# The first stage of a quantized FFN kernel: conditioning of block 1 moved into the first product, and three smaller rearrangements

## What is computed

```python
c = einsum('bct,bcd->bdt', x, cond_weights[cond])      # x: (128, 64, 512)
h = gelu(einsum('bsd,hd->bsh', c, ternarize(W1)) + b1) # W1: (2048, 512)
y = einsum('bsd,hd->bsh', h, ternarize(W2)) + b2       # W2: (512, 2048)
scale = max|y| / 7 + 1e-8
out = x + clip(round(y / scale), -7, 7) * scale

def ternarize(W):
    delta = 0.05 * max|W|;  mask = |W| > delta
    n = max(sum(mask), 1);  alpha = sum(|W| where mask) / n
    return alpha * sign(W) * mask
```

## Time and profile before

| | |
|---|---|
| median of 3 runs | 1014.92 us (1014.45 to 1015.22) |
| profiled execution | 1013.76 us |
| its span | 1012.0 us |
| PE busy | 928.2 us, 92% |
| DVE busy | 647.5 us, 64% |
| ACT busy | 546.2 us, 54% |
| mean granted clock of PE | 0.97 |

### The profile page before, as it was taken

The page is one execution under the profiler, slowest core; times in us unless marked ns, Lnnn a source line. Parts: engine busy times, 40 slices in busy tenths (PEclk is TensorE's granted clock), DMA queues, the critical chain, the costliest instruction groups (busy, mean ns, idle before and its releaser), DMA issues.

```text
span 1012.0 us, 14566 instructions
## 1 busy us (share of the span) xinstructions
PE 928.2 (92%) x5088; PEld 439.1 (43%) x5088; DVE 647.5 (64%) x1025; ACT 546.2 (54%) x688; POOL 145.4 (14%) x187
## 2 busy tenths in 40 slices
PE   2899999999999999999999999999999999999600
PEld 2354444444444444444444444444444444444200
DVE  7999666566667666665667666565666665633492
ACT  5685826455472827446372827446372826535290
POOL 1420030210303030110303030110303030000000
PEclk9999999999999999999999999999999999999855
DMA  9401201111210301121210301121210301105899
GB/s 347 136 9 38 46 11 42 47 47 41 52 41 17 76 10 41 46 47 41 52 41 10 83 10 41 45 48 41 52 41 10 75 18 42 42 0 201 300 394 391
DMA packets 24317, 77.85 MB, mean 77 GB/s; under 512 B 3952, under 2 KB 4080, under 8 KB 23792
## 3 DMA queue, kind: packets, MB, share of 16 engines
q1 hardware_dynamic: 20032, 73.41, 24.1%
q0 software_dynamic: 3840, 3.94, 1.4%
q10 hardware_dynamic: 432, 0.34, 0.1%
HBM read 60.89 MB, written 16.78 MB: 77 GB/s over the span
## 4 chain that ended last, share of the span: by engine, by line
PE 83%; issue 9%; DVE 4%; ACT 1%; DMA 1%; DVEq 0%; POOL 0%; POOLq 0%
PE ps L426 41%; PE ps L436 36%; PE ps L491 3%; PE ps L406 3%; ACT y L680 1%; DVE st L814 1%; DVE wts L1017 1%; DMA condb<-in_itok_B 1%; DVE y L1017 0%; DVE y L833 0%; PE ps L414 0%; PE ps L454 0%; DVE yc L746 0%; DVEq L58 0%; DVE st L697 0%
## 5 line engine op out<-in xcount | busy, mean ns | idle before, releaser
L426 PE MATMUL ps<-yc,wts 128*128 128x512 f16 x2048 | 446.3, 380 | 3.6 <-DVE yc L746 3.6
L436 PE MATMUL ps<-wts 128*128 128x512 f16 x1792 | 391.4, 379 | 0.0
L426 PEld LDWEIGHTS ps<-yc,wts 128*128 128x128 f16 x2048 | 200.7, 98 | 246.8 <-DVE yc L746 4.1
L730 DVE SCALAR_TENSOR_TENSOR wts<-g,st,wts 128x512 f16<-128x512 f32 x256 | 186.3, 749 | 144.0 <-ACT wts L593 142.4
L588 ACT ACTIVATE g<-ps,b1t,st 128x512 f32<-128x512 f32 x256 | 197.9, 773 | 129.0 <-PE ps L426 120.7
L436 PEld LDWEIGHTS ps<-wts 128*128 128x128 f16 x1792 | 173.4, 98 | 204.9
L593 ACT ACTIVATE wts<-g,st 128x512 f16<-128x512 f32 x256 | 180.8, 712 | 0.0
L575 ACT ACTIVATE xs<-yx,st 128x2048 f16<-128x2048 f32 x28 | 56.1, 2002 | 135.5 <-DVE st L764 135.5
L359 POOL PARTITION_ALL_REDUCE st<-st x46 | 22.7, 494 | 672.5 <-DVE st L699 412.7
L343 POOL DMA_INDIRECT wg<-in_L_cond_weights,ids x112 | 110.0, 982 | 41.5 <-issue 29.1
L735 DVE SCALAR_TENSOR_TENSOR y<-ps,st,b2b 128x512 f32 (+1 forms) x56 | 41.6, 747 | 78.9 <-PE ps L436 78.1
(11 more groups left out here) (127 smaller groups left out, 359.3 us busy)
## 6 DMA issues: line engine op xcount, KB each, us to landing
yx<-in_x SPq DMA_DIRECT2D x56, 512.0 KB, 6.2
out<-wts SPq DMA_DIRECT2D x12, 512.0 KB, 14.9
wts<-in_x SPq DMA_DIRECT2D x10, 512.0 KB, 5.6
y<-in_L_ffn_W SPq DMA_DIRECT2D x8, 512.0 KB, 8.6
wts<-in_x SPq DMA_DIRECT2D x4, 1024.0 KB, 5.2
y<-in_L_ffn_W SPq DMA_DIRECT2D x4, 1024.0 KB, 18.5
y<-in_x SPq DMA_DIRECT2D x4, 1024.0 KB, 10.7
out<-y SPq DMA_DIRECT2D x4, 1024.0 KB, 15.3
```

The costliest lines, as they stand in the source:

```text
L426: last = nc.tensor.matmul(psH[:, j % HB, :], T1T[:, j // HC, k, j % HC * P:(j % HC + 1) * P], csp[:, a, k, :], start=(k == 0 and a == 0), ...
L436: last = nc.tensor.matmul(psY[:, r % 2, :], hsp[:, a, j, r * P:(r + 1) * P], T2T[:, j, :], start=(j == 0 and a == 0), stop=(j == HT - 1 an ...
L730: nc.vector.scalar_tensor_tensor(out=hsp[:, 1, j, :], in0=g[:, j % HB, :], scalar=s_h, in1=hsp[:, 0, j, :], op0=ALU.mult, op1=ALU.subtract ...
```

## The change

It edits the first stage on all engines:

- DVE: the two memsets (`wdirect`, `twos`) go ahead of the wait for the conditions.
- x of block 0 is bounded by a sum of absolute values over each partition, made by ACT (`ACT.Abs` with `accum_out`), in place of DVE's maximum. The all-reduce on POOL waits for it (`x0_summed`). A factor in `mr[:, 1:2]` follows from the new bound.
- POOL: two of the four gathers for block 1 go right behind those of block 0, two behind the all-reduce of W1's maximum. SP: x of block 1 is loaded ahead of W2.
- PE: block 1 is conditioned behind j = 0 of block 0's first product, into the banks that block 0's conditioning used; its copy goes to a place of its own (`cf1`) and is made by ACT after tiles 3 and 5. Behind the first product only waits remain.
- PE: `count2` takes W2's negatives (`neg2`) as the stationary operand in 64 pieces of 128 columns and one column of the constant as the moving one; the result is one column.
- ACT: `relu1` and `spread_w(1)` are ordered anew; the first pair of `relu2` goes inside `hidden(0)` after j = 11, the others directly behind it, and `high_c(1)` behind those.
- DVE: two `ternary1` go ahead of the scale of h, the maxima of W2 alternate with `low_h`, `scale_xw` goes to the end of the alpha2 sequence, and `low_x(0, 0)` behind the stores and maxima of y of block 0.

The diff, cut to these parts:

```diff
@@ sync
             load_direct(0)
+            load_direct(1)
             load_weight(w2s, W2.rearrange("p j n -> p (j n)"), WCH, w2_loaded)
-            load_direct(1)
             load_half(0, 2 * DIRECT)
@@ gpsimd
-            gather_direct(0)
+            gather_direct(0, range(RT))
+            gather_direct(1, range(0, 2))
...
             all_max(max1_part, 1, m1r, m1, max1_all)
+            gather_direct(1, range(2, RT))
+            pool.wait_ge(x0_summed, 1)
             all_max(xwb_part, 1, xwbr, xwb, xwb_all)
-            gather_direct(1)
...
             all_max_c(1)
-            all_max(xw_part, 1, xwr, xw, xw_all)
             pool.wait_ge(sum2_part, 1)
             nc.gpsimd.partition_all_reduce(sum2r, sum2, P, RADD).then_inc(sum2_all, 1)
+            all_max(xw_part, 1, xwr, xw, xw_all)
@@ tensor
             def count2(c):
-                for n in range(WCH):
-                    last = nc.tensor.matmul(psN2, twos[:, :], quarter(neg2, c, n), start=(c == 0 and n == 0),
-                                            stop=(c == WCH - 1 and n == WCH - 1))
+                for n in range(QUARTER // P):
+                    at = c * QUARTER + n * P
+                    last = nc.tensor.matmul(psN2, neg2[:, at:at + P], twos[:, 0:1], start=(c == 0 and n == 0),
+                                            stop=(c == WCH - 1 and n == QUARTER // P - 1))
...
                 first(0, j, wait_bank=j >= HB, wait_c=False)
-
-            pe.wait_ge(xdirect_loaded[1], 16)
-            pe.wait_ge(w_spread, 2)
-            condition_direct(1, 0, psC)
-            pe.wait_ge(g_made, HT - 2)
-            condition_direct(1, 1, psC1)
-
+                if j == 0:
+                    pe.wait_ge(xdirect_loaded[1], 16)
+                    pe.wait_ge(w_spread, 2)
+                    condition_direct(1, 0, psC)
+                    condition_direct(1, 1, psC0)
+
+            pe.wait_ge(c_copied, 2)
             pe.wait_ge(g_made, HT)
@@ scalar
+            nc.scalar.activation(dump_x, xdirect[0].rearrange("p r t -> p (r t)"), ACT.Abs, accum_out=xwb[:, 0:1])\
+                .then_inc(x0_summed, 1)
...
-            hidden(0, lambda j: spread_w(1) if j == 3 else None, wait_c=False)
-            act.wait_ge(delta2_ready, 1)
-            act.wait_ge(t1_made, WCH)
-            for side in range(2):
-                relu2(0, side)
-            act.wait_ge(h_split, HT)
-            copy_c_direct(1, 0, psC[:, :, :])
-            copy_c_direct(1, 1, psC1)
+            def beside_first(j):
+                if j in (3, 5):
+                    copy_c_direct(1, (j - 3) // 2, (psC, psC0)[(j - 3) // 2])
+                if j == 11:
+                    act.wait_ge(delta2_ready, 1)
+                    act.wait_ge(t1_made, WCH)
+                    for side in range(2):
+                        relu2(0, side)
+
+            hidden(0, beside_first, wait_c=False)
@@ vector
-            dve.wait_ge(xdirect_loaded[0], 16)
-            nc.vector.tensor_reduce(xwb[:, 0:1], xdirect[0], AX.XY, ALU.max, apply_absolute_value=True).then_inc(xwb_part, 1)
...
-            ternary1(1)
+            ternary1(3)
             low_h(0, 0)
-            ternary1(2)
-            low_h(0, 1)
...
+            for c in range(WCH):
                 last = max_w2(c)
+                low_h(0, 2 * c + 1)
+                if c < WCH - 1:
+                    low_h(0, 2 * c + 2)
...
-            low_x(0, 0)
+            scale_xw(0, 0, link)
             dve.wait_ge(b2_loaded, 16)
...
             for r in range(RT):
                 max_y(0, r, tile_y(r), slot(r), wait_last=r > 0)
+            low_x(0, 0)
             hidden_step(0, link, False)
```

More of the change, by code:

```diff
@@ L132, in build @@
         w1s, w1abs, w2s = flat(y[:, 0:4, :, :]), flat(y[:, 4:8, :, :]), flat(y[:, 8:12, :, :])
-        mask1, neg2, dump2 = f16(y[:, 12:14, :, :]), f16(y[:, 4:6, :, :]), f16(y[:, 0:4, :, :])
+        mask1, neg2, dump2 = f16(y[:, 12:14, :, :]), f16(y[:, 6:8, :, :]), f16(y[:, 0:4, :, :])
         t1_flat, t2_flat = wts[:, 0:KT * H], wts[:, KT * H:2 * KT * H]
@@ L143, in build @@
         cf = g[:, :, :]
+        cf1 = y[:, 4, :, :]
+        dump_x = hsp[:, 0, 0:RT, :].rearrange("p j r -> p (j r)")
         def place(ap):
@@ L181, in build @@
         n1, n1c, sm1, alpha1, alpha1p = stat(), stat(), stat(), stat(), stat()
-        rs2, at2 = stat(2 * WCH), stat(WCH)
+        rs2, at2 = stat(2 * WCH), stat(WCH + 1)
         sum2, sum2r = stat(2), stat(2)
@@ L185, in build @@
         cinv = stat(2)
-        n2n, n2, n2c, sm2, alpha2 = stat(), stat(), stat(), stat(), stat()
+        n2c, sm2, alpha2 = stat(), stat(), stat()
         pm, ms, mr = stat(KT), stat(2), stat(2)
@@ L199, in build @@
         psC0 = psY[:, :, :].rearrange("p i (k r) -> p (i k) r", k=KT // 2)
-        psC1 = psH[:, 0:2, :].rearrange("p i (k r) -> p (i k) r", k=KT // 2)
-        psN1, psN2 = psH[:, HB - 1, :], ps[:, HB, :]
+        psN1, psN2 = psH[:, HB - 1, :], ps[:, HB, 0:1]
         psY0 = [psY[:, 0, :], psY[:, 1, :], psH[:, 2, :], psH[:, 3, :]]
@@ L219, in build @@
         xwb_part, xwb_all = sem("xwb_part"), sem("xwb_all")
+        x0_summed = sem("x0_summed")
         mask1_made = sem("mask1_made")
@@ L345, in gather, with gather_direct @@
                         in_offset=bass.IndirectOffsetOnAxis(ap=ids[:, j:j + 1], axis=0)).then_inc(w_gathered[j // HALF], 16)
-            def gather_direct(b):
-                for r in range(RT):
+            def gather_direct(b, tiles):
+                for r in tiles:
                     nc.gpsimd.indirect_dma_start(
@@ L484, in _ @@
                 if j == 3 * HC:
-                    pe.wait_ge(c_copied, 1)
                     for c in range(WCH):
@@ L557, in copy_c_direct @@
                 act.wait_ge(c_made, 2 * b + half + 1)
-                nc.scalar.activation(cf[:, :, half_rows(half)], bank, ACT.Copy).then_inc(c_copied, 1)
+                nc.scalar.activation(cf1[:, :, half_rows(half)], bank, ACT.Copy).then_inc(c_copied, 1)
             def high_c0(half, bank):
@@ L576, in high_x, with high_c @@
                 nc.scalar.activation(ws[:, 0, js, :], wg[:, js, :], ACT.Copy, scale=sxw[:, 1:2]).then_inc(xhi_made, 1)
-            def high_c(b):
+            def high_c(b, cf=cf):
                 act.wait_ge(cscale_ready, b + 1)
@@ L622, in relu2 @@
                                      accum_out=rs2[:, 2 * c + side:2 * c + side + 1]).then_inc(relu2_summed, 1)
-            for c in range(6):
+            for c in range(LOADS):
                 absolute(c)
+            act.dma_start(b2b[:, :], b2.rearrange("(a n) -> a n", a=1).to_broadcast([P, T])).then_inc(b2_loaded, 16)
             act.wait_ge(diagonal_cleared, 1)
             spread_w(0)
-            for c in range(6, LOADS):
-                absolute(c)
-            act.dma_start(b2b[:, :], b2.rearrange("(a n) -> a n", a=1).to_broadcast([P, T])).then_inc(b2_loaded, 16)
+            act.wait_ge(xdirect_loaded[0], 16)
+            nc.scalar.activation(dump_x, xdirect[0].rearrange("p r t -> p (r t)"), ACT.Abs, accum_out=xwb[:, 0:1])\
+                .then_inc(x0_summed, 1)
             act.wait_ge(delta1_ready, 1)
             act.wait_ge(w1abs_made, LOADS)
-            for c in range(3):
-                relu1(c)
+            relu1(0)
             high_c0(0, psC)
             high_c0(1, psC0)
+            relu1(1)
+            act.wait_ge(c_made, 2)
+            spread_w(1)
+            relu1(2)
             relu1(3)
             act.wait_ge(relu_summed, WCH)
-            hidden(0, lambda j: spread_w(1) if j == 3 else None, wait_c=False)
-            act.wait_ge(delta2_ready, 1)
-            act.wait_ge(t1_made, WCH)
-            for side in range(2):
-                relu2(0, side)
-            act.wait_ge(h_split, HT)
-            copy_c_direct(1, 0, psC[:, :, :])
-            copy_c_direct(1, 1, psC1)
[L649 to L652, removed]
+            def beside_first(j):
[7 more added lines that the diff above has]
+            hidden(0, beside_first, wait_c=False)
+            for c in range(1, WCH):
                 for side in range(2):
                     relu2(c, side)
+            act.wait_ge(h_summed, HT)
+            high_c(1, cf1)
             high_x(0, 0)
@@ L693, in bits, with max_c @@
                 return ap.bitcast(I32)
-            def max_c(b, lk):
+            def max_c(b, lk, cf=cf):
                 dve.wait_ge(c_copied, 2 * b)
@@ L716, in scale_h, with low_c @@
                 nc.vector.tensor_scalar(ascale, pc, 2.0 / TOP, alpha1, ALU.mult, ALU.mult).then_inc(hscale_ready, 1)
-            def low_c(b):
+            def low_c(b, cf=cf):
                 dve.wait_ge(cscale_ready, b + 1)
@@ L796, in _ @@
             link(nc.vector.tensor_tensor(pc64, upper, pcol, ALU.add))
+            nc.vector.memset(wdirect, 0.0).then_inc(diagonal_cleared, 1)
+            nc.vector.memset(twos[:, :], 2.0).then_inc(consts_made, 1)
             dve.wait_ge(cond_loaded, 16)
@@ L841, in _ @@
             mask_w1(0)
```

(49 more changed lines are left out.)

2 lines of the change are left out of this document (removed).

## The result

The changed kernel takes 1020.68 us (median of 4 runs, 1020.26 to 1021.5) against 1014.68 for the kernel before (4 runs): ratio 1.0067, 95% interval 1.0055 to 1.008, so 5.6 to 8.1 us slower. The ratio is not the quotient of these two medians (1.0059): it agrees with the mean of these 4 runs over that of the 19 runs of the kernel before that stand beside the first experiments (median 1013.84). The profiled execution took 1020.87 us, 7.11 more than the one before.

The account below looks back on a forecast made before the run. The prediction took TensorE, busy 92% of the span, to bound the kernel nearly everywhere. It summed +0.4 - 1.6 + 5.25 + 1.3 = +5.35 us, giving 1020.3 us against the median of 1014.92, range 1016.0 to 1024.0.

Parts of the forecast that it names:

- Likeliest case: Whole kernel: all terms as summed, 1020.3 us, own range 1018 to 1022.5; chance 0.60.
- start of the second product: Block 0: second product starts at 66.55 us against 66.13, +0.4 us; ends -0.8 (delta2 then binds) to +1.2 (POOL late).
- the count: Counting W2's negatives on PE: 64 one-column matmuls at 29 ns take 1.86 us instead of 3.45, -1.6 us.
- clock behind the gap before the second product: Block 0's second product: no clock loss behind a 3.05 us gap, as shorter than 3.61; 0, bounds 0 and 1.86 us.
- stall at j = 10: Block 1's first product: PE waits for gelu 6, 7.5 us delay less 2.25 slack, +5.25 us (4.7 to 5.5).
- clock behind it: Block 1's first product, behind the j = 10 gap: slow clock costs 1.3 us, bounds 0 and 1.86.
- The front: Up to block 0's first product: -0.66 for memsets, -2.27 for x's maximum, +0.25 delay; start at 30.4 instead of 33.08 us.
- The uncovered gap: Before block 0's second product: without the moved conditioning, gelus behind two relu2 passes leave PE waiting 3.05 us.
- x of block 2: Block 1's first product: later low_x(0, 0) delays x_split, transfer and reduce by 7.5 us, stalling PE 5.25 us.
- the late x is hidden: Rival, block 1's first product: PE isn't held at j = 10; total 1013.7 us, or 1012.5; chance 0.13.
- weight loads are unhidden: Rival, count of W2's negatives: +2.8 us instead of -1.6, total 1024.7 us; chance 0.12.
- a clock that falls after both new gaps: Rival, second product and block 1's first product: +1.86 and +1.86 us instead of 1.3, total 1022.7; chance 0.15.

Follow-up runs that it names:

- front_only: Kernel before with only the early memsets, ACT's absolute passes first and block 0's x bounded by ACT's Abs sum: 1010.12 us against 1013.59, ratio 0.9964.
- relu2_behind: Changed kernel with the first pair of relu2 behind block 0's first product instead of inside it: 1016.8 us against 1013.84 for the kernel before, ratio 1.0031.
- fill_gap: Changed kernel with 14 unread matmuls of 512 columns ahead of the second product's wait for the gelus: 1018.58 us against 1013.84 for the kernel before, ratio 1.0045.
- lowx_only: Kernel before with only low_x(0, 0) moved behind the four stores and four maxima of y of block 0: 1021.78 us against 1013.84, ratio 1.0075.
- late_max: Changed kernel with next x's maximum, scale, low_x and ACT's high_x placed later in block 1's first product: 1012.1 us against 1013.84 for the kernel before, ratio 0.9981.
- lowx_mid: Changed kernel with low_x(0, 0) between block 0's four stores and four maxima of y: 1016.12 us against 1013.3 for the kernel before, ratio 1.0022.
- repaired: Changed kernel with late_max, relu2_behind and cast 9 of h ahead of W2's first ternary quarter on DVE: 1008.28 us against 1013.59 for the kernel before, ratio 0.9947.
- count_only: Kernel before with only W2's negatives counted by 64 one-column products, their sum moved into the all-reduce of sum2: 1011.7 us against 1013.59, ratio 0.9982.

## Why the prediction was right, and where it wasn't

Likeliest case and sign held: 1020.3 forecast, 1020.68 measured. That the total is so near is in part luck. The forecast adds +5.35 us to the median before, which lay 1.16 us above the profiled execution; the profiled execution of the changed kernel lies 0.19 us above its own median. By the ratio the change costs 6.8 us, by the profiled executions 7.1, so the size was 1.5 to 1.8 us short. By the prediction's own steps, from the profiled executions:

| term | forecast | measured |
|---|---|---|
| start of the second product (66.13 before) | +0.4 | -1.29 |
| the count | -1.6 | -1.87 |
| clock behind the gap before the second product | 0 | +1.85 |
| stall at j = 10 | +5.25 | +5.93 |
| clock behind it | +1.3 | +2.4 |
| sum | +5.35 | +7.0 |

**The front.** 30.4 forecast, 30.38 measured, with two errors inside that cancel:

```profile
20.60 2.41 POOL L352 DMA_INDIRECT wg<-in_L_cond_weights,idsd  x1 [0.30 <-issue]
...
23.05 0.33 POOL L363 PARTITION_ALL_REDUCE st<-st  x1
```

The second gather took 2.41 us, not 1.68 at most, and held the all-reduce back to 23.05; but the all-reduce took 0.33 us where up to 1.23 was allowed, and DVE went on at 23.41. What failed is the sentence that PE idles from 26.6 to 30.4 and pays 1.86 us again. I had moved the masks of W1 forward and not the conditioning ahead of them on PE: it ends only at 25.6, and the 16 products that count W1, before split in 12 and 4, run behind it in one piece. The gap in front of the first product was 1.15 us, and its eight matmuls before the moved conditioning took 1.90 us, at full clock:

```profile
25.61 3.62 PE L452 MATMUL ps<-y,twos 128*128 128x512 f16 x16
30.38 1.90 PE L431 MATMUL ps<-yc,wts 128*128 128x512 f16 x8 [1.15 <-DVE yc L757]
```

front_only shows the same apart: with a gap of 2.25 us the first product lost no clock. That moves the second product's start by the 1.7 us between the forecast and the measurement. The -1.29 us also lie outside the ends that the prediction gave this term, -0.8 to +1.2 us. The lower end took it that delta2 binds once the first product loses no clock; it didn't. delta2 was ready at 55.5 us, not 56.8, and relu2 followed gelu 11's cast without waiting for it:

```profile
55.33 0.14 DVE L907 TENSOR_SCALAR st<-st 128x1 f32<-128x1 f32 x1
55.56 0.71 ACT L598 ACTIVATE wts<-g,st 128x512 f16<-128x512 f32 x1
...
56.17 1.99 ACT L626 ACTIVATE y<-y,st 128x2048 f16<-128x2048 f32 x1
```

**The uncovered gap.** Its place, its releaser (gelus behind the two relu2 passes) and its size (3.05 forecast, 3.09 measured) were right. The view names no releaser for this gap ("issue"); the last gelu ends at 64.74, 0.1 us before PE starts, and relu2_behind and fill_gap show the parts. That such a gap lets the clock fall, which I priced at nothing for being shorter than 3.61 us, was wrong, at 1.85 us. By chance the two errors on the clock cancel.

**The count.** Right, and a little cheaper: 25 ns against 29. The Trainium skill's page "TensorE: Matmul & The Clock Gate", section "LDWEIGHTS (loading the stationary operand)", gives the estimate of 107 ns for a load. That is near what the traces list for one, 98 ns in the earlier trace rows and 96 ns here. What doesn't hold is adding 64 of them up to 6.8 us, since they overlap in PE's weight-load row:

```profile
87.03 1.86 PEld L460 LDWEIGHTS ps<-twos,y 128*128 128x128 f16 x64
```

The same page's section "Wait — 56ns, not 53.3ns?" states a floor of about 25 ns from start to start for small matmuls, which the trace agrees with (1.58 us for 64).

**x of block 2.** The mechanism held at each step, and lowx_only, late_max and lowx_mid each show it apart. The mis-sized term is the time from x_split to the reduce: 7.46 us from the one row that had it, 111.33 - (102.84 + 0.48) = 8.0 here and 107.57 - (99.67 + 0.48) = 7.4 in lowx_mid, for the same two transfers. That is 0.55 of the 0.7 us. Over the seven runs with a late x_split the same stretch took 7.3 to 8.8 us (repaired 7.29, late_max 8.77), so one row couldn't fix it, and 4.7 to 5.5 was too narrow a range for the stall. What spreads it stays open. The larger error is the clock behind this gap: 2.4 us where 1.86 was the upper bound, taken from the one slow stretch before.

**The rivals.** That the late x is hidden fell with lowx_only; that weight loads are unhidden fell with the count's 1.58 us. The rival of a clock that falls after both new gaps is what happened, inside a sum that was near the likeliest case's because the first product no longer paid.

What stays open: whether the clock falls behind a gap between 2.37 and 3.08 us, for which no run here has a case, and how often it falls behind each of the others, since no gap was seen in more than three traces.

## What to carry to other kernels

When work is taken out from between two stages because it fits elsewhere, ask what it covered there: here block 1's conditioning hid the last gelu, and ACT's extra passes made 3 us of what was uncovered (0.92 us in repaired). Follow a moved instruction to the transfer that its semaphore starts, and from there to the next instruction that waits for it in a fixed order; if that one can be placed later (late_max, 8 us for four numbers), the late transfer is free. Put a cheap filler or the next stage's work into gaps of PE such as those of 3 us and more here, since they cost 1.5 to 2.6 us beyond themselves.

## What the runs showed of the hardware that I had not expected

Idle gaps of PE ahead of a product and what the granted clock did behind them, in the one profiled execution of each kernel: none of 1.15, 1.74, 2.25 and 2.37 us was followed by a slow stretch; all of 3.08 (late_max), 3.09, 3.61, 5.24, 5.31, 5.59 and 5.93 us were, at a loss of 1.5 to 2.6 us (against the same pieces behind a short gap: 20.88, 10.53 and 27.80 us). The same gap of 3.61 us cost 29.49 - 27.80 = 1.7 us in two executions (before, count_only) and 30.40 - 27.80 = 2.6 in a third (lowx_only). Filling a gap with products that nobody reads gave 1.7 us back. And 128x128 f16 weight loads, each with a one-column product, follow each other every 25 ns, with 64 columns every 29 ns, though one load is listed with 96 to 98 ns.
